# Counts of the bisection steps under the heads: summed by VectorE from a row in HBM instead of by a matmul, with the move behind q and k's low parts

## The chip, the cores and the metric

One core of a Trainium2 chip runs the program. The metric is the device time of one execution in microseconds, the median of several runs. TensorE does matmuls, VectorE and ScalarE elementwise work and reductions along a row, GpSimd casts and splits, SyncE issues most of the DMAs; ScalarE has a DMA queue of its own. Each engine takes its instructions in the order in which they are written, and they meet through semaphores.

## What is computed

```python
x = x + top_k_mask(s * cond * softmax(x) / sqrt(512), diagonal = -inf, k = 5120)   # one 0/1 matrix of 512 x 512 per sequence
ada = (cond @ ada_w + ada_b)                     # shift1, scale1, gate1, shift2, scale2, gate2
x1 = ln(x) * (1 + scale1) + shift1
q, k, v = x1 @ qkv_w + qkv_b                     # 16 heads of 128
a = softmax(q @ k.T / sqrt(128)) @ v @ out_w + out_b
y = x + gate1 * a
y = y + gate2 * (gelu((ln(y) * (1 + scale2) + shift2) @ ffn_w1 + ffn_b1) @ ffn_w2 + ffn_b2)
out = x + y
```

B is 4 sequences of T = 512 rows and D = 512 columns. The mask marks the 5120 largest of the 262,144 values of a sequence.

## The kernel before

The four sequences ("blocks" 0 to 3) are worked one after another: v and then 16 heads of attention, the output projection, and the two layers of the MLP. Every product of float32 is made of three matmuls over high and low parts (`mm3`, L1395 to L1397), so every operand is split in two: on ScalarE the high part is written, on VectorE the low part (`q_hi`, `q_lo` and so on).

In block 0 the weights come raw from HBM (`wraw`), ScalarE casts the high half (L819, `split_hi`), GpSimd makes the low half (L660, `split_lo`), and SyncE saves the pair to `split_weights` in HBM, from which the later blocks load it (L466). In head 3, 7 and 11 of block 0 two more casts than usual stand on ScalarE's queue (`refill`), for the v weights of the next four heads or for the output projection.

**One head h of block b.** TensorE: scores of h (12 matmuls in 4 banks), the total of a bisection step where there is one, the projection of q and k for head h + 1 (24), the v tile of head h + 4 or, from head 12 on, a piece of the output projection, and the product of head h - 1's probabilities with v (`attend`). VectorE: four row maxima (L1217) and biases (L1219), the sums' inverses (L1230, L1232), the low halves of the probabilities (L1236), low parts of q and k for h + 1 (L1187), v's low part (L1182), the low part of head h - 1's output (o, L1187). ScalarE: four exponentials (L883), the probabilities' high halves (L890), q and k (L871, L875), v (L867), o (L910). SyncE turns the halves by DMA transposes (L537), and GpSimd widens them to float32 (L740) for `attend`. All engines go from head to head without a barrier; o of head h - 1 waits for the product, which is the last thing on TensorE in head h, and the first row maximum of h + 1 stands behind it on VectorE.

**The bisection.** The k-th largest value of sequence b + 1 is found under block b, by 32 steps. One step: VectorE counts how many of its half of the keys pass the candidate `cand` (`count`, L1027), ScalarE does so for the other half (`topk_count`, L778), each leaving a number per partition in `counts` (128 x 2). TensorE sums these over the partitions with a matmul against ones (`take_total`, L1411), and VectorE moves the candidate by three small operations (`topk_move`, L1094 to L1099), which both counts of the next step wait for. Steps 0 to 10 (`HEAD_STEPS` is 11) lie under heads 4 to 15: counted at the end of a head, totalled by TensorE behind the scores of the next head, moved by VectorE between that head's biases and its sums. Steps 11 to 31 lie in the stages behind the heads, at places of a table (`SLOTS`); the first of them, `("out", 1, 2)`, is on TensorE shortly behind head 15. The last block has no bisection under it, and block 0's own one runs ahead of all blocks.

## Time and profile before

| | |
|---|---|
| median of 3 runs | 1549.21 us (1548.57 to 1549.74) |
| profiled execution | 1549.28 us, span 1547.5 us |
| TensorE busy | 1499.1 us, 97% |
| VectorE busy | 1107.3 us, 72% |
| ScalarE busy | 884.3 us, 57% |
| GpSimd busy | 424.2 us, 27% |
| DMA | 327.65 MB, mean 212 GB/s |
| granted TensorE clock | 1.00 |

The span is the profiled execution without what lies around it. A head takes about 13.7 us, and 64 heads are more than half of the span. Starts in the rows below are us from the span's start. TensorE's matmuls overlap in the rows: their distance is read from starts, not from durations.

### The profile page before, as it was taken

Reading aid. Unit: us, or ns where it says so; the run is one execution under the profiler, and the core shown is the slowest. Engines: PE = TensorE matmul, PEld = TensorE weight load, DVE = VectorE, ACT = ScalarE, POOL = GpSimd, SP = SyncE. Lnnn points to the kernel's source line nnn. Section 1 sums busy time; section 2 is a strip of 40 time slices with the busy share of each in tenths; the row PEclk is TensorE's granted clock in tenths of the full one; section 3 lists DMA queues with packets and bytes.
Section 4 is the critical chain, followed back from the end, with each engine's and each line's share of the span. In section 5 each row is a group of like instructions: output and inputs, shape, how many; then the busy total and the mean of one; then the engine's idle time right before and its main releaser. Section 6 shows DMA issues by size and latency. Waiting matters only on the chain.

```text
span 1547.5 us, 22147 instructions
## 1 busy us (share of the span) xinstructions
PE 1499.1 (97%) x7157; PEld 1244.7 (80%) x7157; DVE 1107.3 (72%) x2572; ACT 884.3 (57%) x1631; POOL 424.2 (27%) x371
## 2 busy tenths in 40 slices
PE   1999999999999999999999999999999999999998
PEld 1878788879788888888878887888878888888987
DVE  7878887777796887876784887876786666664431
ACT  4656777765846566662753666663572655554340
POOL 6714555554021422331000432232000232223000
PEclk9999999999999999999999999999999999999999
DMA  7866899996767677775465788686465686776463
GB/s 293 300 265 191 230 225 267 255 250 241 257 247 246 172 198 202 207 188 182 172 225 217 196 208 197 155 215 206 164 232 190 191 218 160 196 214 158 182 238 118
DMA packets 338611, 327.65 MB, mean 212 GB/s; under 512 B 274848, under 2 KB 279104, under 8 KB 335424
## 3 DMA queue, kind: packets, MB, share of 16 engines
q1 hardware_dynamic: 338208, 325.91, 71.0%
q8 instruction: 57, 0.93, 0.2%
q14 instruction: 58, 0.48, 0.1%
q10 hardware_dynamic: 288, 0.33, 0.1%
HBM read 204.54 MB, written 54.54 MB: 167 GB/s over the span
## 4 chain that ended last, share of the span: by engine, by line
PE 90%; DVE 4%; DVEq 1%; DMA 1%; ACT 1%; issue 1%; SPq 1%; POOL 0%; ACTq 0%; POOLq 0%
PE bank L1395 27%; PE bank L1397 27%; PE bank L1396 27%; PE bank L1717 2%; PE bank L1615 1%; PE bank L1610 1%; PE bank L1611 1%; DVE tb L1027 1%; PE bank L1427 1%; DVEq L1218 1%; DMA w<-split_weights 1%; SPq L537 1%; PE bank L1449 1%; PE bank L1446 1%; PE bank L1445 1%
## 5 line engine op out<-in xcount | busy, mean ns | idle before, releaser
L740 POOL CAST probT<-turned 128x1024 fp32r<-128x1024 f16 x256 | 260.1, 1053 | 679.5 <-PE bank L1397 355.0
L1395 PE MATMUL bank<-xT,w 128*128 128x512 f32 x704 | 279.7, 397 | 0.0
L1396 PE MATMUL bank<-xT,w 128*128 128x512 f32 x704 | 273.9, 389 | 0.0
L1397 PE MATMUL bank<-xT,w 128*128 128x512 f32 x704 | 273.8, 389 | 0.0
L883 ACT ACTIVATE prob<-bank,nbias 128x512 f32<-128x512 f32 x256 | 176.2, 689 | 107.9 <-DVE nbias L1219 98.8
L1236 DVE SCALAR_TENSOR_TENSOR halves<-prob,rinv,halves 128x512 f16<-128x512 f32 x256 | 176.0, 750 | 27.2 <-ACT halves L890 27.2
L890 ACT ACTIVATE halves<-prob,rinv 128x512 f16<-128x512 f32 x256 | 163.8, 712 | 30.6 <-DVE rinv L1232 23.9
L1217 DVE TENSOR_REDUCE rowmax<-bank 128x1 f32<-128x512 f32 x256 | 174.4, 681 | 0.0
L1397 PEld LDWEIGHTS bank<-xT,w 128*128 128x128 f32 x704 | 132.2, 188 | 28.0
L1395 PEld LDWEIGHTS bank<-xT,w 128*128 128x128 f32 x704 | 132.9, 189 | 25.0
L1396 PEld LDWEIGHTS bank<-xT,w 128*128 128x128 f32 x704 | 132.4, 188 | 24.9
L660 POOL TENSOR_TENSOR w<-wraw,w 128x1024 fp32r<-128x1024 f32 x38 | 94.0, 2478 | 178.8 <-ACT w L819 177.6
L1395 PE MATMUL bank<-act,w 128*128 128x512 f32 (+1 forms) x320 | 113.4, 354 | 0.0
L1397 PE MATMUL bank<-act,w 128*128 128x512 f32 (+1 forms) x320 | 111.0, 347 | 0.0
L1396 PE MATMUL bank<-act,w 128*128 128x512 f32 (+1 forms) x320 | 111.0, 347 | 0.0
L778 ACT ACTIVATE passed_s<-adj,cand 128x1024 bf16<-128x1024 uint16 (+1 forms) x64 | 73.8, 1153 | 62.5 <-DVE cand L1099 37.4
L1187 DVE SCALAR_TENSOR_TENSOR act<-bank,small,act 128x512 fp32r<-128x512 f32 x64 | 47.9, 748 | 85.4 <-ACT act L910 85.4
L910 ACT ACTIVATE act<-bank,small 128x512 fp32r<-128x512 f32 x64 | 44.0, 688 | 106.3 <-PE bank L1397 106.3
L778 ACT ACTIVATE passed_s<-low,cand 128x1024 bf16<-128x1024 f32 (+1 forms) x64 | 74.0, 1156 | 51.0 <-DVE cand L1099 24.1
L1395 PE MATMUL bank<-qk 128*128 128x512 f32 x256 | 100.1, 391 | 1.7 <-DVE qk L1187 1.2
L1395 PE MATMUL bank<-w,act 128*128 128x512 f32 x256 | 101.5, 397 | 0.0
L1187 DVE SCALAR_TENSOR_TENSOR qk<-bank,small,qk 128x512 fp32r<-128x512 f32 x128 | 90.2, 744 | 14.2 <-ACT qk L875 7.9
(171 smaller groups left out, 3314.7 us busy)
## 6 DMA issues: line engine op xcount, KB each, us to landing
w<-split_weights SPq DMA_DIRECT2D x154, 1024.0 KB, 5.6
split_weights<-w SPq DMA_DIRECT2D x38, 1024.0 KB, 6.8
wraw<-weights_in SPq DMA_DIRECT2D x48, 512.0 KB, 4.8
split_weights<-xT SPq DMA_DIRECT2D x7, 1024.0 KB, 8.0
adaw<-ada_w_in SPq DMA_DIRECT2D x4, 1536.0 KB, 13.0
xr<-x_in SPq DMA_DIRECT2D x4, 1024.0 KB, 5.7
turned<-halves SPq DMA_TRANSPOSE x256, 3.3
split_weights<-qk SPq DMA_DIRECT2D x3, 1024.0 KB, 7.6
```

Source lines behind the costliest of these rows:

```text
L660: nc.gpsimd.tensor_tensor(w[:, region, 1, span], wraw[:, k % 2, :], w[:, region, 0, span].bitcast(F32), ALU.subtract)\
L740: nc.gpsimd.tensor_copy(probT[:, :, :, i * P:(i + 1) * P].rearrange("p a j t -> p (a j) t"), turned_of(h)[:, i, :, :]).then_inc(widened, 1)
L778: nc.scalar.activation(passed_s[:, :2 * NCOUNT - at], src, ACT.Sign, bias=cand[:, :], scale=-1.0, accum_out=cnt_s[:, :]).then_inc(counted_ ...
L883: nc.scalar.activation(prob[:, i, :], bank[i][:, :], ACT.Exp, bias=nbias[:, i:i + 1], scale=SCALE, accum_out=rowsum[:, i:i + 1]).then_inc( ...
L890: nc.scalar.mul(halves_of(h)[:, i, 0, :], prob[:, i, :], rinv[:, i:i + 1]).then_inc(p16_hi, 1)
L910: nc.scalar.activation(act[:, 0, h, :], bank[6][:, :], ACT.Identity, bias=col("bv", h))\
L1187: return V.scalar_tensor_tensor(dst, src, bias, hi.bitcast(F32), ALU.add, ALU.subtract)
L1217: V.reduce_max(rowmax[:, i:i + 1], bank[i][:, :], AX.X)
L1236: V.scalar_tensor_tensor(halves_of(h)[:, i, 1, :], prob[:, i, :], rinv[:, i:i + 1], halves_of(h)[:, i, 0, :], ALU.mult, ALU.subtract).then ...
L1395: pe.matmul(dst, w_hi_ap, x_hi_ap, start=first, stop=False)
L1396: pe.matmul(dst, w_hi_ap, x_lo_ap, start=False, stop=False)
L1397: return pe.matmul(dst, w_lo_ap, x_hi_ap, start=False, stop=last)
```

## The change

Under the heads of blocks 0 to 2 the total is no longer a matmul. When both counts of a step are there, ScalarE sends `counts` (128 partitions x 2 numbers of 2 bytes) to a row `count_rows` in HBM, behind head h - 1's o. Behind the exponentials of the next head it waits for that send and fetches the row into all partitions (`all_counts`, 128 x 256 numbers, 512 bytes each). VectorE sums the 256 numbers to two (`summed`), and moves the candidate as before. The move stands no longer between the biases and the sums, but behind q and k's low parts, directly ahead of the count of the next step. TensorE's matmul of the total and its two waits (for o's low part and for the candidate) are gone from the heads. The steps behind the heads stay as they were.

```diff
+        all_counts = at("all_counts", [P, P, 2], F16, passed_at)
+        summed = new("summed", [P, 2], F32)
+        count_rows = nc.dram_tensor("count_rows", (P, 2), F16, kind="Internal").ap()
...
+            def send_counts(t, step):
+
+                act_e.wait_ge(counted_v, t * STEPS + step + 1)
+                act_e.wait_ge(counted_s, t * STEPS + step + 1)
+                act_e.dma_start(count_rows, counts[:, :]).then_inc(counts_out, 16)
+
+            def fetch_counts(t, step):
+
+                act_e.wait_ge(counts_out, 16 * ((t - 1) * HEAD_STEPS + step + 1))
+                act_e.dma_start(all_counts[:, :, :].rearrange("p n c -> p (n c)"),
+                                count_rows.rearrange("n c -> (n c)").unsqueeze(0).to_broadcast([P, 2 * P]))\
+                    .then_inc(counts_in, 16)
...
                     nc.scalar.activation(prob[:, i, :], bank[i][:, :], ACT.Exp, bias=nbias[:, i:i + 1],
                                          scale=SCALE, accum_out=rowsum[:, i:i + 1]).then_inc(exp_done, 1)
+                if not last and h >= FIRST_TOTAL:
+                    fetch_counts(b + 1, h - FIRST_TOTAL)
...
                 if h:
                     o_part(b, h - 1)
+                if not last and 0 <= h + 1 - FIRST_TOTAL < HEAD_STEPS:
+                    send_counts(b + 1, h + 1 - FIRST_TOTAL)
                 refill(b, h, 1)
...
             def topk_move(t, step):
-                dve.wait_ge(total_ready, t * STEPS + (step + 1))
-
+                if is_t0(t):
+                    dve.wait_ge(total_ready, step + 1)
+                    sums = total(step)
+                elif step < HEAD_STEPS:
+                    dve.wait_ge(counts_in, 16 * ((t - 1) * HEAD_STEPS + step + 1))
+                    V.tensor_reduce(summed[:, :], all_counts[:, :, :].rearrange("p n c -> p c n"), AX.X, ALU.add)
+                    dve.drain()
+                    sums = summed
+                else:
+                    dve.wait_ge(total_ready, t * (STEPS - HEAD_STEPS) + step + 1)
+                    sums = total(step)
...
-                if FIRST_TOTAL <= h and not last:
-                    topk_move(b + 1, h - FIRST_TOTAL)
                 keys_first = is_first(b) and 0 < h < FIRST_TOTAL
...
                 if h + 1 < H:
                     qk_part(b, h + 1)
                 dve.drain()
+                if FIRST_TOTAL <= h and not last:
+                    topk_move(b + 1, h - FIRST_TOTAL)
                 if not last and not keys_first:
                     topk_under_head(b + 1, h)
...
-                step = h - FIRST_TOTAL
-                if 0 <= step < HEAD_STEPS and not last:
-                    pe.wait_ge(o_lo, b * H + h)
-                    take_total(b + 1, step)
                 if h + 1 < H:
                     qk_proj(b, h + 1)
...
                 pe.wait_ge(o_lo, b * H + (h + 1))
-                if 0 <= step < HEAD_STEPS:
-                    pe.wait_ge(cand_ready, (b + 1) * (STEPS + 1) + (step + 2))
```

VectorE in a head from 5 on, before: from the last bias to the count.

```order
L1219 TENSOR_SCALAR nbias<-rowmax 128x1
L1094 TENSOR_SCALAR step_up<-bank 128x1 [waits total_ready]
L1097 TENSOR_SCALAR step_up<-bank,step_up 128x1
L1099 TENSOR_SCALAR cand<-cand,step_up 128x1
L1230 TENSOR_SCALAR rowsum<-rowsum 128x1 [waits exp_done]
L1230 TENSOR_SCALAR rowsum<-rowsum 128x1
L1232 RECIPROCAL rinv<-rowsum 128x2
```

The same engine and head after the change, from the sums' inverse to the next row maximum.

```order
L1260 RECIPROCAL rinv<-rowsum 128x2
L1264 SCALAR_TENSOR_TENSOR halves_0_69<-prob,rinv,halves_0_69 128x512 [waits p16_hi] x4
L1217 SCALAR_TENSOR_TENSOR qk<-bank,small,qk 128x512 [waits q_hi]
L1217 SCALAR_TENSOR_TENSOR qk<-bank,small,qk 128x512 [waits k_hi]
L1111 TENSOR_REDUCE summed<-all_counts 128x2 [waits counts_in]
L1124 TENSOR_SCALAR step_up<-summed 128x1
L1127 TENSOR_SCALAR step_up<-summed,step_up 128x1
L1129 TENSOR_SCALAR cand<-cand,step_up 128x1
L1048 TENSOR_SCALAR tb,counts<-adj,cand 128x1024
L1212 SCALAR_TENSOR_TENSOR v<-bank,v 128x512 [waits v_hi]
L1217 SCALAR_TENSOR_TENSOR act<-bank,small,act 128x512 [waits o_hi]
L1247 TENSOR_REDUCE rowmax<-bank 128x1 [waits scores]
```

The three operations of the move now stand behind the low parts of q and k, with a sum of 256 numbers ahead of them, and the count, v's and o's low parts stand behind them.

ScalarE after the change, one head of block 1. Before, the same rows stood there without the two DMA rows.

```order
L931 ACTIVATE act<-bank,small 128x512 [waits pv_done]
L789 DMA count_rows<-counts 128x2 [waits counted_s,counted_v]
L900 ACTIVATE prob,rowsum<-bank,nbias 128x512 [waits nbias_ready] x4
L794 DMA all_counts<-count_rows 128x256 [waits counts_out]
L909 ACTIVATE halves_0_69<-prob,rinv 128x512 [waits turned_in3,turned_in2,rinv_ready,turned_in1,turned_in0]
L909 ACTIVATE halves_0_69<-prob,rinv 128x512 [waits rinv_ready] x3
L888 ACTIVATE qk<-bank,small 128x512 [waits q_done]
L892 ACTIVATE qk<-bank,small 128x512 [waits k_done]
L782 ACTIVATE passed_s,counts<-adj,cand 128x1024 [waits cand_ready]
L884 ACTIVATE v<-bank 128x512 [waits v_done]
```

The send stands behind o and ahead of the exponentials, the fetch between these and the halves; the count (L782) keeps its place on ScalarE, but the candidate that it waits for is now made behind q and k's low parts.

TensorE before, behind the scores of a head; after the change the row of L1411 is gone and the projection follows the scores.

```order
L1395 MATMUL bank<-qk 128x512
L1396 MATMUL bank<-qk 128x512
L1397 MATMUL bank<-qk 128x512
L1411 MATMUL bank<-counts,ones 128x2 [waits counted_s,counted_v,o_lo]
L1395 MATMUL bank<-xT,w 128x512 [waits w_in10]
L1396 MATMUL bank<-xT,w 128x512
```

What moved on this engine: nothing but the total, and the first matmul of `attend` has lost its wait for `cand_ready`.

## Rows read from the trace of the kernel before

**Rows 1.** Part 1 of the page: busy time, share of the span, instructions.

```profile
PE 1499.1 (97%) x7157; PEld 1244.7 (80%) x7157; DVE 1107.3 (72%) x2572; ACT 884.3 (57%) x1631; POOL 424.2 (27%) x371
```

**Rows 2.** Stretches: first score matmul to the next; block 1, twice last; all heads.

```profile
core 0: us, PE busy (x) PEld busy (x) DVE busy (x) ACT busy (x) POOL busy (x), PEclk, DMA share, GB/s
577.35:591.08 13.73, 13.73 (x62) 11.21 (x61) 10.87 (x27) 9.26 (x18) 4.01 (x4) 1.00 0.62 150
1284.53:1298.13 13.60, 13.60 (x61) 11.27 (x60) 9.18 (x22) 8.00 (x16) 4.01 (x4) 1.00 0.66 165
1366.13:1379.05 12.92, 12.92 (x58) 10.70 (x57) 8.49 (x21) 7.40 (x15) 4.01 (x4) 1.00 1.04 307
484.60:685.17 200.57, 200.57 (x890) 164.46 (x889) 164.45 (x405) 133.48 (x266) 59.92 (x60) 1.00 0.76 198
119.11:324.97 205.86, 202.35 (x890) 163.88 (x889) 167.86 (x405) 150.64 (x287) 109.62 (x81) 1.00 0.93 239
```

**Rows 3.** Timeline of TensorE around a total: start, duration, engine, line, operation.

```profile
579.84 0.39 PE L1397 MATMUL bank<-qk 128*128 128x512 f32 x1
...
580.43 0.39 PE L1396 MATMUL bank<-xT,w 128*128 128x512 f32 x1
```

**Rows 4.** Timeline of VectorE, head 7 of block 1.

```profile
587.07 1.41 DVE L1187 SCALAR_TENSOR_TENSOR qk<-bank,small,qk 128x512 fp32r<-128x512 f32 x2
588.59 1.28 DVE L1027 TENSOR_SCALAR_CACHE_REDUCE tb<-adj,cand 128x1024 bf16<-128x1024 uint16 x1
```

**Rows 5.** Timeline of VectorE and ScalarE, head 7 of the last block.

```profile
1299.72 0.68 DVE L1217 TENSOR_REDUCE rowmax<-bank 128x1 f32<-128x512 f32 x1
...
1303.84 2.55 ACT L890 ACTIVATE halves<-prob,rinv 128x512 f16<-128x512 f32 x4
...
1307.24 1.41 DVE L1187 SCALAR_TENSOR_TENSOR qk<-bank,small,qk 128x512 fp32r<-128x512 f32 x2
```

**Rows 6.** Timeline of VectorE and ScalarE, a move behind the heads.

```profile
702.66 0.16 DVE L1094 TENSOR_SCALAR step_up<-bank 128x1 f32<-128x1 f32 x1 [2.06 <-PE bank L1411]
...
703.44 1.15 ACT L778 ACTIVATE passed_s<-adj,cand 128x1024 bf16<-128x1024 uint16 x1 [2.97 <-DVE cand L1099]
```

**Rows 7.** DMAs: issue on ScalarE's queue; size, median us to landing.

```profile
0.79 0.39 ACTq L993 DMA_DIRECT2D small<-cols_in  x1
...
turned<-halves SPq DMA_TRANSPOSE x256, 3.3
...
small<-cols_in ACTq DMA_DIRECT2D x1, 64.0 KB, 1.8
gate_rows<-gate_t SPq DMA_DIRECT2D x1, 16.0 KB, 5.9
```

**Rows 8.** Timeline, block 0: TensorE's wait in head 4, heads 5 and 7, v tile.

```profile
184.06 0.50 PE L1395 MATMUL bank<-w,xT 128*128 128x512 f32 x1 [1.77 <-POOL w L660]
...
196.39 0.72 ACT L890 ACTIVATE halves<-prob,rinv 128x512 f16<-128x512 f32 x1 [1.71 <-DMA turned<-halves]
199.96 0.74 DVE L1187 SCALAR_TENSOR_TENSOR qk<-bank,small,qk 128x512 fp32r<-128x512 f32 x1
200.94 1.15 ACT L778 ACTIVATE passed_s<-adj,cand 128x1024 bf16<-128x1024 uint16 x1
203.96 0.68 DVE L1217 TENSOR_REDUCE rowmax<-bank 128x1 f32<-128x512 f32 x1
...
228.26 1.05 ACT L819 CAST w<-wraw 128x1024 fp32r<-128x1024 f32 x1
231.73 4.01 POOL L740 CAST probT<-turned 128x1024 fp32r<-128x1024 f16 x4
235.70 2.40 POOL L660 TENSOR_TENSOR w<-wraw,w 128x1024 fp32r<-128x1024 f32 x1
239.17 0.39 PE L1395 MATMUL bank<-w,xT 128*128 128x512 f32 x1
```

**Rows 9.** Timeline of VectorE and TensorE behind head 15 of block 1.

```profile
696.57 0.09 DVE L1027 DVE_READ_ACCUMULATOR tb<-adj,cand 128x1 f16 x1
...
698.23 0.18 PE L1411 MATMUL bank<-counts,ones 128*128 128x2 f16 x1
```

More of the change, by code:

```diff
@@ L373, in block_kernel @@
                                                        sem("adj_ready"), sem("diag_done"))
+        counts_out, counts_in = sem("counts_out"), sem("counts_in")
         cand_ready, counted_v, counted_s, total_ready = (sem("cand_ready"), sem("counted_v"),
@@ L1084, in topk_move @@
             def topk_move(t, step):
-                dve.wait_ge(total_ready, t * STEPS + (step + 1))
+                if is_t0(t):
[9 more added lines that the diff above has]
+                    sums = total(step)
                 bit = TOP_BIT / (1 << step % LEVEL)
                 if is_t0(t):
-                    move = V.tensor_scalar(cand[:, :], total(step)[:, 0:1], bounds[:, 0:1], bounds[:, 1:2],
+                    move = V.tensor_scalar(cand[:, :], sums[:, 0:1], bounds[:, 0:1], bounds[:, 1:2],
                                            ALU.max, ALU.min)
@@ L1093, in topk_move @@
                     bit *= unit(step)
-                    V.tensor_scalar(step_up[:, :], total(step)[:, 1:2], 0.5, float(KTOP - P * NCOUNT // 2) - 0.5,
+                    V.tensor_scalar(step_up[:, :], sums[:, 1:2], 0.5, float(KTOP - P * NCOUNT // 2) - 0.5,
                                     ALU.mult, ALU.add)
                     dve.drain()
-                    V.tensor_scalar(step_up[:, :], total(step)[:, 0:1], step_up[:, :], bit, ALU.is_gt, ALU.mult)
+                    V.tensor_scalar(step_up[:, :], sums[:, 0:1], step_up[:, :], bit, ALU.is_gt, ALU.mult)
                     dve.drain()
@@ L1527, in head, with attend @@
                 if h:
-                    attend(b, h - 1, step if not last else -1)
-            def attend(b, h, step):
+                    attend(b, h - 1)
+            def attend(b, h):
                 q, m = h // QUAD, h % QUAD
@@ L1679, in sequence @@
                 wide(b, "out", 0, KC - 2, KC - 1, y_done)
-                attend(b, H - 1, -1)
+                attend(b, H - 1)
                 wide(b, "out", 2, 0, 3, y_done)
```

## The prediction

> **What bounds the kernel now.** I read the page first: TensorE is busy 97% of the span [rows 1], so a removal counts only where it takes time out of TensorE's row of matmuls, and a delay elsewhere costs only once TensorE waits for it. Then the stretches of single heads [rows 2]. A head of block 1 takes 13.73 us from one first score matmul to the next, and TensorE is busy in all of it. The same head in the last block, where no bisection runs under the heads, takes 13.60. Sixty matmuls of 0.2265 us (the distance of starts) are 13.59, so the last block is TensorE at its pace. The difference of 0.13 to 0.14 us is the total: between the matmul before it (579.84) and the second one behind it (580.43) lie 0.59 us, where two plain steps are 0.45 [rows 3]. Heads 12 to 14, three matmuls shorter, take 12.92 without totals. The granted clock is 1.00 in all these stretches.
>
> **What the change takes away.** 3 blocks x 11 heads (5 to 15) lose one total each: 33 x 0.135 = 4.5 us, all on TensorE's own path. The waits of TensorE for the counts and for the candidate in these heads go too; block 1's heads have no idle time of TensorE [rows 2], so they are worth nothing.
>
> **What it adds, and where it lies.** I follow one loop, from a head's first rowmax to the next head's first rowmax on VectorE, since VectorE and ScalarE take turns on it.
> Rowmax to the low parts of q and k: the last block has no move there and shows 1299.72 to 1307.24, 7.52 us, with ScalarE's halves starting 4.12 behind the rowmax [rows 5]. So with the move gone from its old place the halves of all heads come that early.
> Low parts to the next VectorE instruction: 587.07 to 588.59, 1.52 [rows 4].
> The new sum of 256 numbers: not in the trace. Below, a 128x1 operation is 0.16 [rows 6]; above, a reduction of 512 is 0.68 [rows 5]. I take 0.44 with the handover, half the elements of the upper row and its fixed part.
> Move until ScalarE's count starts: 702.66 to 703.44, 0.78 [rows 6].
> Count on ScalarE, then v, o, and VectorE's rowmax of the next head, with no wait for TensorE among them: 200.94 to 203.96, 3.02 [rows 8].
> Sum 7.52 + 1.52 + 0.44 + 0.78 + 3.02 = 13.28 us, against the 13.60 that TensorE takes. The margin is 0.32 (0.60 to 0.08 over the bounds of the sum): where nothing else comes, the longer loop hides under the matmuls. A head that starts late also has a cushion: TensorE wants q and k's low parts of head 8 at 591.08 and has them at 588.48, 2.6 us early [rows 2, 4].
>
> The two DMAs. The send is queued behind o on ScalarE and ahead of the next exponentials; behind it in the queue stand these, the fetch, the halves. From o to the halves there are about 5.5 us (1.4 with o's low part, the end of the 3.02 above, then 4.12). The two issues were 0.39 us each where ScalarE's queue was otherwise empty [rows 7]; the exponentials last until 0.1 before the halves, so the issues can lie under them if ScalarE's arithmetic goes on while its queue issues. Issue to landing for the 512 bytes: 1.8 us is the lowest row, 3.3 the transposes under the same load, 5.9 the worst small one, queued behind others [rows 7]. I take 3 to 3.5, inside the window of 4.7; likewise the fetch has some 5 us until the sum. So: nothing in blocks 1 and 2.
> The Trainium skill, "Advanced Engine Details and Errata", section Sequencer Loop, says that other engine instructions can be read and queued while the sequencer executes a control instruction. No row of this trace shows a DMA issued by ScalarE beside its arithmetic; by that page the issues are free, and the other answer is the third case below.
>
> **Block 0 is another matter.** Its heads take 205.86 us where block 1 takes 200.57 [rows 2], because ScalarE also casts weights and GpSimd splits them, and the loop arrives late. In head 5 the halves start only at 196.39, held by transposes; low parts follow at 199.96, and ScalarE counts at 200.94, beside them [rows 8]. After the change the count stands behind them and the move: 199.96 + 1.52 + 0.44 + 0.78 = 202.7, 1.76 later. The next rowmax is at 205.7 instead of 203.96, and 0.32 a head gives back little. Head 7: rowmax 219.0, count at 229.3, and the cast of the first half of the next v weights behind v, 1.6 later, at 230.9 instead of 228.26 [rows 8]. Follow it: cast done 231.9, GpSimd's split 2.4 to 234.4, its four casts of probT (before from 231.73) 4.0 to 238.4, the split of the second half (before from 235.70) to 240.8. TensorE asks for that half at 239.17, and with four totals gone at 238.6: 2.2 us of waiting that are not there now. The trace has such a wait once, at 184.06, 1.77 us for the same splits [rows 8]. Heads 11 to 14 repeat the pattern (two casts at head 11, transposes queued behind the weights' loads); there the boundaries are late already, and I take 2.4 us for both together, an estimate from the same lags. Last, the first total behind the heads: in block 1 the counts are done at 696.66 and TensorE comes at 698.23 [rows 9], 1.57 of cushion. Without a lag the new order takes 0.57 of it (the move only changes its place, the sum's 0.44 is new, TensorE comes 0.13 sooner). A lag of about 2.1 us in block 0 then costs 1.1. Block 0: 2.2 + 2.4 + 1.1 = 5.7 us lost.
>
> **The sum** against the profiled run, 1549.28 us (span 1547.5; median of the runs 1549.21): -4.5 + 5.7 = +1.2, **1550.5 us**.
>
> **Rivals.**
> *The gain stays (22%).* If head 5's late start is made good (GpSimd splits in another order of arrival, raw loads land earlier), block 0 loses nothing: 1549.3 - 4.5 = 1544.8. For it: TensorE's row shows no other cost, blocks 1 and 2 have 2.6 us of cushion. Against it: the cast at 230.9 is a plain sum of rows.
> *The issues are not hidden (27%), slower.* If each fetch takes 0.42 us from ScalarE before the halves, the loop is 13.70, above 13.60, and decides from there: VectorE falls back in every head. In blocks 1 and 2 the lag grows by 0.10 in heads 5 to 11 and by 0.3 in heads 12 to 14, whose loop loses only the v part (0.5) while TensorE's stretch loses 0.68 [rows 2]: 1.6 us, within the cushion of 2.6 but not within that of the first total behind the heads: 1.6 + 0.42 - 1.0 is 1.0 us each, 2 in all. In block 0 three heads' issues come on top before each pair of casts and at the end, 3.6 us. Together 1550.5 + 5.6 = 1556.
> The skill's page "Perfetto Trace Analysis", section DMA Instruction (HWDGE), says that one descriptor generator is shared by the issuing sequencers and locked while it is used. SyncE's transposes take 5.5 us of issue for four in every head, so by this page the same case would come from a send or fetch that meets them; no row shows two queues issuing at once.
> *The send lands late (9%).* ScalarE stands at the fetch until the rows have landed, with halves and q, k behind it. From 4.7 us of landing on, each further microsecond is one per head: at 2 us too late 33 x (2 - 0.3) less three times the cushion of 2.6 is 48 us, some 1598. For it speaks only the row of 5.9.
> *Forecast (42%)*, 1548 to 1554 with the bounds of the sum (0.08 to 0.60 of margin) and of block 0's 2.4.
>
> **Range and chances.** A measurement of this kernel can tell about 0.2%, 3.1 us. Faster by more is the first rival, 0.22; within is the forecast, 0.42; slower are the other two, 0.36. The range from 1544 to 1561 takes in the first rival and most of the second, and leaves out about 0.15.
>
> **What would show it.** Head stretches of blocks 1 and 2 of 13.60 and 12.92 us: the total's price is right. ScalarE's halves 4.1 us behind the rowmax, not 4.5 or more: the issues are hidden; an idle time of the halves put down to a DMA to count_rows is the late landing. Idle time of VectorE before the sum would be a late fetch. A gap of 2 us before a v matmul near 239 us, put down to GpSimd's w: block 0's account. I am wrong if block 0 keeps its 205.9 less 1.5, or if the sum takes over 0.76 us with its handover, since the margin is then gone in every head.

## The result: 11.6% slower, and the time is in the send

| | before | after |
|---|---|---|
| median, us | 1549.17 | 1728.56 (1722.99 to 1733.53) |
| span of the profiled run, us | 1547.5 | 1731.5 |
| mean granted clock of TensorE | 1.000 | 0.958 |

The ratio is 1.1155, 95% interval 1.1139 to 1.1172: some 180 us, where 1 was forecast and the range ended 12 above the time of before. In the page of the kernel after, these lines answer to [rows 1] and [rows 7] (busy time; the chain of what ended last, by engine and by line; a group of instructions with what ended its idle time; DMA issues with their median landing):

```profile
PE 1553.3 (90%) x7124; PEld 1280.3 (74%) x7124; DVE 1127.7 (65%) x2605; ACT 884.1 (51%) x1631; POOL 427.9 (25%) x371
...
PE 58%; DMA 21%; DVE 10%; SPq 4%; ACT 2%; DVEq 2%; issue 2%; ACTq 0%; POOL 0%; POOLq 0%
...
L909 ACT ACTIVATE halves<-prob,rinv 128x512 f16<-128x512 f32 x256 | 163.7, 712 | 162.9 <-DMA count_rows<-counts 101.1
...
all_counts<-count_rows ACTq DMA_DIRECT2D x33, 64.0 KB, 5.0
...
count_rows<-counts ACTq DMA_DIRECT2D x33, 0.5 KB, 9.8
```

TensorE's share fell from 97% to 90%, and DMAs make up 21% of the chain (1% before). The send's median landing is 9.8 us, its shortest 7.8; the forecast had taken 3 to 3.5. ScalarE's halves (the high halves of the probabilities) stood idle for 162.9 us (30.6 before), 101.1 of them put down to the send, in 20 of the 33 heads, and 52.3 to transposes of the halves before them (6.7 before). The transposes' median landing is 3.4 us (3.3 before), the longest 14.6 (8.2 before). In the view of stretches, the heads of block 1, single heads of it, the stretch behind them, and the last block (us, TensorE busy, ..., granted clock):

```profile
core 0: us, PE busy (x) PEld busy (x) DVE busy (x) ACT busy (x) POOL busy (x), PEclk, DMA share, GB/s
625.55:642.71 17.16, 13.76 (x62) 11.11 (x60) 9.10 (x23) 8.00 (x16) 4.01 (x4) 1.00 0.45 104
676.87:700.78 23.91, 18.64 (x60) 14.14 (x61) 13.66 (x34) 10.37 (x20) 4.18 (x4) 0.79 1.04 201
560.27:807.08 246.81, 214.48 (x881) 172.90 (x879) 167.37 (x410) 132.03 (x264) 60.77 (x60) 0.94 0.79 162
807.08:975.99 168.91, 162.59 (x825) 135.36 (x826) 113.08 (x243) 79.59 (x132) 11.25 (x12) 0.97 0.58 190
1389.64:1588.88 199.24, 199.24 (x881) 164.98 (x880) 134.74 (x326) 117.26 (x236) 56.31 (x56) 1.00 0.77 200
```

Block 1's heads went from 200.57 us [rows 2] to 246.81; the last block, which sends nothing, is at its pace. A head of 17.16 us has 3.4 us in which TensorE is idle. In the head of 23.91 it is also slower: 60 matmuls keep it busy for 18.64 us at a granted clock of 0.79, behind heads in which it had stood idle, where 62 took 13.73 at 1.00 before. Over the run TensorE's busy time grew by 54 us (1499.1 to 1553.3, with 33 matmuls less) and its time outside that by 130. The three stretches behind the heads, in which nothing is sent, are 28.7 us of the 184 by which the span grew (169.29, 168.91 and 168.87 us against 159.63, 159.26 and 159.48). In each of them TensorE stands idle once for what the last head left late, 6.3, 6.1 and 6.4 us (the first total behind the heads, and in block 2 the probabilities), and is busy for some 3 us more than before at a granted clock of 0.97.

What one head waits for, in the timeline of ScalarE and VectorE in head 7 of block 1 (start, duration; idle time ahead of an instruction and what ended it in brackets):

```profile
662.06 0.58 ACT L884 ACTIVATE v<-bank 128x512 fp32r<-128x512 f32 x1
662.32 0.33 ACTq L789 DMA_DIRECT2D count_rows<-counts  x1
...
667.96 0.19 ACT L900 ACTIVATION_READ_ACCUMULATOR prob<-bank,nbias 128x1 f32 x1
671.42 0.33 ACTq L794 DMA_DIRECT2D all_counts<-count_rows  x1
671.95 1.34 ACT L909 ACTIVATE halves<-prob,rinv 128x512 f16<-128x512 f32 x2 [3.80 <-DMA count_rows<-counts]
...
675.36 1.41 DVE L1217 SCALAR_TENSOR_TENSOR qk<-bank,small,qk 128x512 fp32r<-128x512 f32 x2
676.86 0.42 DVE L1111 TENSOR_REDUCE summed<-all_counts 128x2 f32<-128x256 f16 x1
677.36 0.15 DVE L1124 TENSOR_SCALAR step_up<-summed 128x1 f32<-128x1 f32 x1
```

The send goes out at 662.32 and the fetch can be issued only at 671.42, 9.1 us later; the exponentials have been done since 668.15. The loop behind the landing is as forecast: low parts to the sum 1.50 (1.52), sum and handover 0.50 (0.44). The send is issued while ScalarE computes v, and costs it nothing.

So the place of the loss is plain. Why 512 bytes take 9 us, and whether that wait is the whole loss, is not.

### The profile page after: what moved, and what is told of

Same layout as the page of the kernel before. It is cut to its first block, busy times and chain, and to the rows that moved or that the text cites. A ratio compares the mean times of both kernels' runs of the same rounds, so it can differ in the third digit from the quotient of the medians.

```text
span 1731.5 us, 22204 instructions
## 1 busy us (share of the span) xinstructions
PE 1553.3 (90%) x7124; PEld 1280.3 (74%) x7124; DVE 1127.7 (65%) x2605; ACT 884.1 (51%) x1631; POOL 427.9 (25%) x371
## 4 chain that ended last, share of the span: by engine, by line
PE 58%; DMA 21%; DVE 10%; SPq 4%; ACT 2%; DVEq 2%; issue 2%; ACTq 0%; POOL 0%; POOLq 0%
PE bank L1425 17%; PE bank L1426 16%; PE bank L1427 16%; DMA count_rows<-counts 14%; SPq L541 3%; DVE halves L1264 3%; DMA w<-split_weights 2%; DMA turned<-halves 2%; DVE tb L1048 2%; PE bank L1741 2%; ACT halves L909 1%; DMA all_counts<-count_rows 1%; DMA wraw<-weights_in 1%; PE bank L1639 1%; PE bank L1634 1%
## 5 line engine op out<-in xcount | busy, mean ns | idle before, releaser
L909 ACT ACTIVATE halves<-prob,rinv 128x512 f16<-128x512 f32 x256 | 163.7, 712 | 162.9 <-DMA count_rows<-counts 101.1
L1425 PE MATMUL bank<-qk 128*128 128x512 f32 x256 | 109.3, 427 | 62.5 <-DVE qk L1217 62.0
L782 ACT ACTIVATE passed_s<-adj,cand 128x1024 bf16<-128x1024 uint16 (+1 forms) x64 | 74.0, 1157 | 147.3 <-DVE cand L1129 122.1
L1425 PE MATMUL bank<-probT,v 128*128 128x512 f32 x256 | 107.0, 418 | 27.8 <-POOL probT L744 27.7
L1425 PE MATMUL bank<-act,w 128*128 128x512 f32 (+1 forms) x320 | 116.3, 363 | 12.8 <-DMA w<-split_weights 12.8
L1426 PE MATMUL bank<-act,w 128*128 128x512 f32 (+1 forms) x320 | 113.6, 355 | 0.0
L1427 PE MATMUL bank<-act,w 128*128 128x512 f32 (+1 forms) x320 | 113.5, 355 | 0.0
L1425 PEld LDWEIGHTS bank<-qk 128*128 128x128 f32 x256 | 52.1, 204 | 82.1 <-DVE qk L1217 70.8
L1426 PE MATMUL bank<-qk 128*128 128x512 f32 x256 | 107.2, 419 | 0.0
L1427 PE MATMUL bank<-qk 128*128 128x512 f32 x256 | 107.0, 418 | 0.0
L1426 PE MATMUL bank<-probT,v 128*128 128x512 f32 x256 | 105.5, 412 | 0.0
```

The source lines that it names most:

```text
L782: nc.scalar.activation(passed_s[:, :2 * NCOUNT - at], src, ACT.Sign, bias=cand[:, :], scale=-1.0, accum_out=cnt_s[:, :]).then_inc(counted_ ...
L909: nc.scalar.mul(halves_of(h)[:, i, 0, :], prob[:, i, :], rinv[:, i:i + 1]).then_inc(p16_hi, 1)
L1425: pe.matmul(dst, w_hi_ap, x_hi_ap, start=first, stop=False)
L1426: pe.matmul(dst, w_hi_ap, x_lo_ap, start=False, stop=False)
L1427: return pe.matmul(dst, w_lo_ap, x_hi_ap, start=False, stop=last)
```

## The experiments

### Is it the place of the move? Or the DMAs? (move_only, free_dmas, fetch_late, bench)

*move_only* is the kernel before, with the move in its new place and the total still a matmul, copied out of PSUM at the old place:

```diff
-                    topk_move(b + 1, h - FIRST_TOTAL)
+                    copy_total(b + 1, h - FIRST_TOTAL)
...
+                if FIRST_TOTAL <= h and not last:
+                    topk_move(b + 1, h - FIRST_TOTAL)
                 if not last and not keys_first:
                     topk_under_head(b + 1, h)
```

> The move alone stands behind the low parts of q and k; the total stays TensorE's matmul at its old place, copied out of PSUM by one small VectorE operation at the move's old place, and no DMA is added. Theory A (the time lies in the wait for the send's landing): within 0.5% of the kernel before, 1545 to 1556 us, with block 0 alone slower by 2 to 6 us. Theory B (the later move and count make VectorE and ScalarE's loop longer than TensorE's head): clearly slower in every head from 5 on, 1570 us or more.

Measured: 1551.53 us against 1549.66, ratio 1.0013 (1.0004 to 1.0022). The move's place costs 2 us, so theory B falls.

*free_dmas* is the kernel before with DMAs on which nothing depends: constants sent, and fetched late in the next head.

```diff
+                act_e.dma_start(count_rows[n], ones[:, 0:2]).then_inc(counts_out, 16)
...
+                if not last and h >= FIRST_TOTAL:
+                    fetch_counts(b + 1, h - FIRST_TOTAL)
                 if h:
                     o_part(b, h - 1)
+                if not last and 0 <= h + 1 - FIRST_TOTAL < HEAD_STEPS:
+                    send_counts(b + 1, h + 1 - FIRST_TOTAL)
```

> The kernel before, with a send of 128 x 4 bytes to HBM and a fetch of 512 bytes to all partitions per head as in the change, but of constants, into a row of its own per step; no engine's work needs them: the fetch is issued late in the next head. Theory A (a wait, not the traffic): 1547 to 1553 us, the sends still 8 us or more to landing. Theory C (128 small descriptors each slow the transposes and the weights' loads on the shared DMA engines): 1570 us or more, with transposes well above 3.4 us to landing.

Measured: 1720.68 us, ratio 1.1104 (1.1082 to 1.1126). This was the surprise of the study: nearly the whole loss, though no count is waited for. In the waits of this kernel the same halves now wait for something else, their own transposes:

```profile
L540 SPq DMA_TRANSPOSE turned<-halves x256: 1230/1247/5494, 127.1 to 1584.9; - x128
...
  POOL probT L744: 592.3, 70
  ACT halves L909: 147.9, 25
...
DMA to landing us min/median/max: 3.0/3.6/16.6
```

The second and third lines tell who waited for the transposes, how long in all and how often. Before, ScalarE's halves waited for them 6.7 us in all and the longest landing was 8.2.

*fetch_late* is the change with only ScalarE's wait and fetch moved, from ahead of the halves to ahead of the next count:

> The change with only the fetch moved on ScalarE, from ahead of the probabilities' halves to ahead of the count. Theory A in the form that halves, q and k waiting behind the fetch are what costs: most of the 180 us come back, under 1600 us. Theory A' (the send's 8 to 9 us, the fetch's 3 to 5, sum, move and count are one chain longer than a head wherever the fetch stands): 1690 to 1760 us, the halves again 4.1 us behind the rowmax, and the idle time before VectorE's sum instead.

Measured: 1719.12 us, ratio 1.1093 (1.1070 to 1.1116). The 101 us of the halves' wait are gone (they wait 30.7 for transposes) and 139.5 us of VectorE's wait for all_counts stand in their place. Moving the wait does not help. It doesn't tell what late counts cost by themselves, since the slow sends and their hold on the transposes are in this run too.

*bench* leaves out all of the reference's work and times single DMAs on ScalarE's queue, each landing waited for, on a quiet chip, beside loads of 1 MB, and beside transposes. All three of the following send 128 pieces of 4 bytes: `near` side by side in HBM, `far` 512 bytes apart, `row` into one partition's row in SBUF.

```diff
+                    act_e.dma_start(dram["near", ph], counts[:, :]).then_inc(sems["near", ph], 16)
...
+                    act_e.dma_start(dram["far", ph][:, 0:2], counts[:, :]).then_inc(sems["far", ph], 16)
...
+                    act_e.dma_start(dst["row", ph][0:1, :].rearrange("o (n c) -> o n c", c=2), counts[:, :])\
```

> Measures DMAs of ScalarE's queue by themselves, one at a time, each waited for, six times each: 128 x 4 bytes to one dense row in HBM (near), the same at 512 bytes' distance (far), 128 x 512 bytes to HBM (wide), 128 x 4 bytes into a row of one SBUF partition (row), that row to HBM in one piece (one), and a row of HBM into all partitions (all). First with no other traffic (quiet), then beside loads of 1 MB by SyncE (loads), then beside DMA transposes (turns). All of the reference's work is left out; the output is a copy of x. Theory L (load): near takes 2 to 3 us when quiet and 8 or more beside loads. Theory S (size and target: writes of 4 bytes to one line of HBM): near takes 6 us or more even when quiet, far and row clearly less.

Measured, from the view of its DMAs (median us to landing last):

```profile
near_quiet<-counts ACTq DMA_DIRECT2D x6, 0.5 KB, 7.2
far_quiet<-counts ACTq DMA_DIRECT2D x6, 0.5 KB, 1.4
row_quiet<-counts ACTq DMA_DIRECT2D x6, 0.5 KB, 1.9
...
near_loads<-counts ACTq DMA_DIRECT2D x6, 0.5 KB, 10.8
far_loads<-counts ACTq DMA_DIRECT2D x6, 0.5 KB, 7.8
...
near_turns<-counts ACTq DMA_DIRECT2D x6, 0.5 KB, 8.3
far_turns<-counts ACTq DMA_DIRECT2D x6, 0.5 KB, 1.9
```

The same 128 pieces of 4 bytes land in 7.2 us side by side and in 1.4 when 512 bytes lie between them. Number, size and queue are the same in both: it is where the pieces fall. Load adds 1 to 4 us to the near ones. The far ones aren't always quick either: beside the loads of 1 MB they take 7.8 us, beside the transposes 1.9.

### Which DMA costs, and by what? (sends_only, fetches_only, far_sends, row_route)

The first three are free_dmas with one thing altered. *sends_only* drops the fetches; *fetches_only* keeps the first send alone and fetches its row 33 times; *far_sends* writes every send but the first 512 bytes apart (the fetches of both read the first row).

```diff
-                act_e.dma_start(count_rows[n], ones[:, 0:2]).then_inc(counts_out, 16)
+                act_e.dma_start(far_rows[n][:, 0:2] if n else count_rows[0], ones[:, 0:2]).then_inc(counts_out, 16)
```

> The kernel before with 33 sends of a constant (128 writes of 4 bytes to a dense row of 512 bytes in HBM) on ScalarE's queue where the change sends the counts, ScalarE waiting for the landing late in the next head; nothing is fetched, the totals are the matmul's. Theory L (the small writes themselves are slow, 8 to 13 us, and the turned<-halves transposes that are issued while they are under way land late with them, which holds GpSimd's probT and ScalarE's halves): 1700 to 1725 us, nearly all of what sends and fetches cost together (1720.68), with transposes landing up to 14 to 17 us after their issue. Rival F (the fetch, 128 rows of 512 bytes, is what the others wait for): 1550 to 1570. Rival W (nothing is held on the DMA side, ScalarE's own wait for the landing is what costs): about 1720 too, but transposes would land within 8.2 us as in the kernel before.

> The kernel before with one send at the first step and 33 fetches of that row to all partitions (64 KB each) where they stood beside the matmul totals; nothing depends on what they bring. Theory L: 1549 to 1556 us, transposes as before (median 3.3, longest about 8 us). Rival F: 1690 to 1720.

> The kernel before with the 33 sends and 33 fetches on which nothing depends, but each send writes its 128 pieces of 4 bytes 512 bytes apart, not side by side. Alone on a quiet chip such a send landed in 1.4 us, against 7.2 for the dense row. Theory L (slow because all pieces fall in one 512-byte stretch): 1550 to 1570 us. Rival Y (any 128 small pieces on a second queue disturb the transposes, wherever they go): 1690 to 1720 like the dense ones.

Measured: sends_only 1706.07 us (ratio 1.1011, 1.0979 to 1.1043), fetches_only 1554.39 (1.0033, 1.0022 to 1.0045), far_sends 1555.43 (1.0036, 1.0020 to 1.0052). The dense sends alone cost 156 us. The fetches cost 5, the fetches together with as many sends to another pattern of addresses 6, and most of even that comes with one dense send: both kernels keep the first, and in block 0, where it goes out at 188.77 us in far_sends, ScalarE's halves come late behind it:

```profile
188.77 0.34 ACTq L790 DMA_DIRECT2D count_rows<-ones  x1
201.25 0.72 ACT L910 ACTIVATE halves<-prob,rinv 128x512 f16<-128x512 f32 x1 [6.58 <-DMA turned<-halves]
```

That head takes 19.0 us from exponential to exponential, where it took 13.5; the heads of its blocks 1 and 2 take what they took before. In sends_only the same happens in head after head. Block 1 again, GpSimd's casts of the turned halves and ScalarE:

```profile
666.52 0.33 ACTq L788 DMA_DIRECT2D count_rows<-ones  x1
...
669.38 1.04 POOL L743 CAST probT<-turned 128x1024 fp32r<-128x1024 f16 x1 [0.39 <-DMA turned<-halves]
678.14 1.04 POOL L743 CAST probT<-turned 128x1024 fp32r<-128x1024 f16 x1 [7.71 <-DMA turned<-halves]
...
678.16 2.56 ACT L903 ACTIVATE halves<-prob,rinv 128x512 f16<-128x512 f32 x4 [6.40 <-DMA turned<-halves]
```

Three of the head's four transposes have landed; the fourth, issued about when the send was, lands 11.6 us behind the send's issue. GpSimd's cast and ScalarE's next halves, which write the tile that it reads, wait for it. Of the theories on record, L holds: what is under way beside the dense send is held with it. F and Y fall. So does W, since transposes land up to 15.3 us after their issue, not within 8.2, and ScalarE's own wait for the sends is 1.1 us in the whole run.

*row_route* is the change with the counts sent to one partition's row in SBUF first, from there in one piece to HBM, then fetched:

```diff
-                act_e.dma_start(count_rows, counts[:, :]).then_inc(counts_out, 16)
+                act_e.dma_start(count_row[0:1, :].rearrange("o (n c) -> o n c", c=2), counts[:, :])\
+                    .then_inc(row_made, 16)
...
+                act_e.dma_start(count_rows.rearrange("n c -> (n c)").unsqueeze(0), count_row[0:1, :])\
+                    .then_inc(counts_out, 16)
```

> The change with another way for the counts: sent first to one partition's row in SBUF (128 pieces of 4 bytes), from there in one piece of 512 bytes to HBM (issued between the exponentials), then fetched by all partitions as in the change. Theory L: the transposes land as before, the three landings (about 3.4, 1.9 and 4 us) reach the sum at most about 3 us late, so 1555 to 1600 us. Rival Y (the small pieces disturb wherever they go): above 1690. If both the place of the pieces and their number matter, something between.

Measured: 1611.45 us, ratio 1.0400 (1.0363 to 1.0437), 11 above the top of what was expected: the row send's median landing is 4.8 us in the kernel, not 3.4. The transposes land as before (median 3.3, longest 8.2), and ScalarE's halves wait for none of them. What is left is that three landings in a row are too long for a head: ScalarE waits 30.6 us for the first (18 times) and its halves 28.4 us for the second (12 times).

### Where is the limit, and does it hold others up by itself? (bench2, bench3)

> None of the reference's work (out is a copy of x). First, on a quiet chip, ScalarE's queue writes 128 pieces of 4 bytes, one from each partition, to a row in HBM with the pieces 4, 8, 16, 32, 64, 128, 256 and 512 bytes apart, each landing waited for. Theory L (what is slow is that many pieces fall in one 512-byte stretch): the landing falls stepwise with the spacing, from 7.2 us at 4 bytes towards 1.4 at 512, with 3 to 5 us at 16 to 32 bytes. Rival R (only a shared word or a partly written 64 bytes is slow): everything from 64 bytes on is alike at about 1.4 us, everything below about 7. Then SyncE issues 40 transposes of 128x1024 two deep: alone, beside a chain of sends to the dense row, and beside a chain of sends 512 bytes apart; and the same with loads of 1 MB. Theory L: transposes 3.2 us alone and beside the far sends at most 4, but beside the dense sends a median of 5 to 8 us and more in the longest; loads 6 to 7 us alone and 1 to 3 us more beside the dense sends. Rival Q (transposes are held only where other loads are in flight too): transposes beside the dense sends alone stay near 3.3.

*bench2* first wrote the 128 pieces at eight distances, five times each, one send behind the other. From one issue to the next, which is little more than the landing, it took 7.0 to 8.3 us at 4 bytes, 2.7 to 3.2 at 8, 1.4 to 2.5 at 16 (1.4 in three of five), and 1.4 to 2.0 from 32 bytes on. So there is no step at 512 bytes, where theory L had put it, and none at 64, where R had.

Then it issued 40 transposes two deep, then 12 loads of 1 MB two deep: alone, beside a chain of dense sends, beside a chain of sends 512 bytes apart. SyncE's issues (start, and the us from the first issue to the last):

```profile
218.50 63.67 SPq L294 DMA_TRANSPOSE turn_alone<-hv  x40
284.10 110.67 SPq L294 DMA_TRANSPOSE turn_beside_near<-hv  x40
396.69 64.89 SPq L294 DMA_TRANSPOSE turn_beside_far<-hv  x40
463.52 34.80 SPq L296 DMA_DIRECT2D wb<-src_load_alone  x12
504.91 69.51 SPq L296 DMA_DIRECT2D wb<-src_load_beside_near  x12
601.04 30.00 SPq L296 DMA_DIRECT2D wb<-src_load_beside_far  x12
```

Eight dense sends of 512 bytes add 47 us to 40 transposes and double the time of the loads (the median load lands in 13.6 us, not 6.8). The 24 far sends add 1.2 us to the transposes and nothing to the loads. Rival Q falls, since no load is needed beside the transposes. Theory L had the median of the transposes wrong: it stays at 3.3 us, since eight sends meet only some of the 40, and those land up to 11.7 us after their issue.

> None of the reference's work (out is a copy of x). On a quiet chip, 128 pieces, one from each partition, of 4, 8, 16, 32 and 64 bytes lying side by side in HBM, and pieces of 4 bytes every 8, 16 and 32 bytes (earlier: 7 us side by side, 2.9, 2.1 and 1.9). Theory N (what costs is two pieces that share 8 bytes: the memory is written 8 bytes at a time or more, one after the other): 8 bytes side by side lands in about 2.9 us and 16 in about 2.1, like pieces of 4 bytes at those distances. Theory Z (every piece of under 64 bytes costs the same read and write back, and only the distance decides): the same figures. Theory B (the small piece itself is slow, whatever lies beside it): 8 bytes side by side 2.9 or more, 16 side by side under 2. If pieces of 8 and 16 bytes side by side are as slow as those of 4 (6 to 8 us), it is the touching, not the distance. Beside them, 24 transposes of 128x1024 two deep take about 38 us alone: 50 to 66 beside the 4 bytes side by side, and 38 to 42 beside the others.

*bench3*, pieces from 128 partitions, by size and distance:

```profile
four_side_by_side<-counts ACTq DMA_DIRECT2D x6, 0.5 KB, 7.5
eight_side_by_side<-counts ACTq DMA_DIRECT2D x6, 1.0 KB, 2.9
sixteen_side_by_side<-counts ACTq DMA_DIRECT2D x6, 2.0 KB, 1.4
...
four_every_eight<-counts ACTq DMA_DIRECT2D x6, 0.5 KB, 2.8
four_every_sixteen<-counts ACTq DMA_DIRECT2D x6, 0.5 KB, 1.5
four_every_thirtytwo<-counts ACTq DMA_DIRECT2D x6, 0.5 KB, 1.4
```

Size makes no difference (4 bytes every 8 are as fast as 8 side by side), nor does touching, and since 4 bytes every 16 land in 1.5 us, this run's theory B falls. What counts is the distance of the pieces' starts: 7.5 us at 4 bytes, 2.9 at 8, about 1.4 from 16 on. Theories N and Z give the same figures and aren't told apart. Every send had 128 pieces, so the distance and the length of the whole stretch grow together here, and fewer pieces weren't tried.

The transposes beside them did not go as expected. From the first to the last issue, 24 of them take 70.4 us beside six sends side by side (50 to 66 expected), with medians of 5.5 and 5.1 us to landing and the longest over 10, and 46.0 beside eight sends 8 bytes apart (38 to 42 expected), with landings up to 6.2. Beside ten sends 16 bytes apart they take 39.9, and beside ten of 16 bytes side by side 39.3. So pieces 8 bytes apart still hold others, only less.

### The change without its slow send (apart16, apart8)

The same kernel as the change, with the pieces 16 (or 8) bytes apart; the fetch brings the gaps along, and the sum reads every fourth (second) pair. SyncE fills the row once at the start, so that the gaps hold numbers.

```diff
-        all_counts = at("all_counts", [P, P, 2], F16, passed_at)
+        all_counts = at("all_counts", [P, P, 8], F16, passed_at)
...
-                act_e.dma_start(count_rows, counts[:, :]).then_inc(counts_out, 16)
+                act_e.dma_start(count_rows[:, 0:2], counts[:, :]).then_inc(counts_out, 16)
```

> The change with one thing altered: the 128 pieces of 4 bytes lie 16 bytes apart in HBM, not side by side, so the fetch brings 2 KB to each partition (256 KB, landed in 3.2 us alone) and VectorE sums every fourth pair. Alone such a send landed in 2.1 us, against 6.9 to 7.5 side by side. If the send's landing was the one step of the forecast that failed, its other steps hold here: a landing of up to 4.7 us from the low parts costs nothing, the fetch has about 5 us, 33 heads win 0.135 us each and block 0 loses about 6: 1549 to 1558 us, heads 5 to 14 of blocks 1 and 2 at a pace of 13.6 us as in the last block, transposes as before. If the length of the route itself (two landings in a row) is too long for a head, whatever the spacing: 1575 to 1620, as with the route through SBUF (1611).

> The same with pieces 8 bytes apart: alone the send landed in 2.9 us, the fetch of 1 KB to each partition in about 3. If the landing alone decides: 1549 to 1565 us, at most some us above the one with 16 bytes. If pieces that share a few bytes' neighbourhood still hold the transposes: 1580 or more, with transposes over 9 us.

Measured: apart16 1566.35 us, ratio 1.0105 (1.0088 to 1.0122); apart8 1585.37, ratio 1.0226 (1.0184 to 1.0268). One number of the layout takes back 162 of the 179 us. Both lie above what was expected, by 8 and 20 us (apart8 has two runs only, 10 us apart, 1580.15 and 1590.58). With 8 bytes the send lands in 5.0 us in the kernel, not 2.9, and late transposes still hold the halves a few times (5.0 us in all, the longest landing 8.9).

In most heads of apart16 the loop can at last be seen as it was forecast. Head 6 of block 2 as a stretch, and ScalarE and VectorE in it:

```profile
939.54:953.14 13.60, 13.60 (x61) 11.26 (x60) 11.68 (x29) 9.13 (x20) 4.00 (x4) 1.00 0.72 178
```

```profile
940.00 0.33 ACTq L791 DMA_DIRECT2D count_rows<-counts  x1
...
941.58 0.68 DVE L1249 TENSOR_REDUCE rowmax<-bank 128x1 f32<-128x512 f32 x1
...
945.07 0.33 ACTq L796 DMA_DIRECT2D all_counts<-count_rows  x1
...
945.68 2.55 ACT L911 ACTIVATE halves<-prob,rinv 128x512 f16<-128x512 f32 x4
...
950.58 0.60 DVE L1113 TENSOR_REDUCE summed<-all_counts 128x2 f32<-128x256 f16 x1
...
952.03 1.15 ACT L784 ACTIVATE passed_s<-adj,cand 128x1024 bf16<-128x1024 uint16 x1 [2.65 <-DVE cand L1131]
...
955.06 0.68 DVE L1249 TENSOR_REDUCE rowmax<-bank 128x1 f32<-128x512 f32 x1
```

The halves start 4.10 behind the rowmax, with a fetch issued under the exponentials; nothing in this head waits for a landing; TensorE is busy in all of 13.60 us, where it took 13.73. The loop from rowmax to rowmax is 13.48.

## Why the prediction was wrong, point by point

**The step that failed** is the send's landing: "I take 3 to 3.5, inside the window of 4.7". It was 8 to 13 us. The bounds were rows of one 64 KB load in large pieces, transposes, and a small save of 16 KB; none of these writes pieces 4 bytes apart, and the one of 5.9, already beyond the window, was put aside as queued. On a quiet chip the send takes 7.2, so no reading of the load could have saved the step.

**The third rival had the wait, at 9%, and half of the mechanism.** It said that an idle time of the halves put down to count_rows would show it, and 101.1 us of that are there. Its price was for 2 us too late; by its own rule, (9.8 - 4.7 - 0.3) x 33 less its 7.8 us, the time would be 1550.5 + 151 = 1701. That this comes near 1728.56 is in part luck: the halves wait for counts in 20 heads, not 33, and the rule leaves out the other half of the mechanism. The send holds the transposes and loads beside it, and costs 156 us even where nobody wants the counts (sends_only). Late counts and held transposes together cost 179, so the counts add 23 at most. Late counts with the transposes as before are in row_route only, at 62 us, and there they come by another way; what a wait for a landing of 9.8 us would cost by itself is not shown.

**The total's price, 0.135 a head, is right.** apart16 has heads of 13.60 and 12.92 us; but 0.135 x 33 is 4.5 us, and nothing else in the change is seen to give time back.

**The loop of 13.28 is right.** In the kernel after, its parts are 1.50, 0.50 and about 0.77, against 1.52, 0.44 and 0.78. In apart16 the strided sum takes 0.60 instead of 0.42, and the loop is 13.48, still under 13.60. In heads 13 and 14, which have no v, it is 12.97 to 13.14 in blocks 1 and 2, against TensorE's 12.92: VectorE can fall behind there by up to 0.2 us a head.

**The fetch's window is a second step that failed, a smaller one.** The forecast gave the fetch "some 5 us until the sum" and no price. In the kernel after its median landing is 5.0 us, and VectorE's sum waits for it 14.2 us in all, in 10 heads. In apart16, where it brings 2 KB to each partition, the median is 3.7 but the longest 7.0; the sum waits 7.2 us in all, in 6 heads, in head 12 of blocks 1 and 2 for 1.50 and 1.44. In apart8 it waits 15.7 us, in 13 heads. In block 1, and TensorE's wait for the first total behind its heads:

```profile
671.16 0.60 DVE L1113 TENSOR_REDUCE summed<-all_counts 128x2 f32<-128x256 f16 x1 [1.50 <-DMA all_counts<-count_rows]
...
713.00 0.16 PE L1443 MATMUL bank<-counts,ones 128*128 128x2 f16 x1 [2.42 <-DVE tb L1050]
```

From that head on VectorE is late: in blocks 1 and 2 the first rowmax of head 15 stands 3.9 us behind its score matmuls where it stood 1.6. The three stretches behind the heads grow from 159.63, 159.26 and 159.48 us to 162.5, 163.3 and 162.0. That is 9.4 of the 16.8 us by which apart16's span is longer, 6.9 of them TensorE's waits for the first total (2.0, 2.4 and 2.5); the forecast had 1.1 for it, in block 0 alone. The heads of blocks 1 and 2 together are 1.4 us shorter than before, where it had 3. Of the missing 1.6 us, 1.4 are a wait of TensorE for a weights' load in head 8 of block 1; what made that load late isn't shown.

**The issues are hidden**, so the second rival (27%) falls. The send's row at 662.32 lies inside v's, and in apart16 the fetch's, at 945.07, inside the last exponential. This is what the Trainium skill, "Advanced Engine Details and Errata", section Sequencer Loop, leads one to expect. The lock on the shared descriptor generator that the Trainium skill describes in "Perfetto Trace Analysis", section DMA Instruction (HWDGE), and on which that rival leaned, is not seen as a cost here. In fetches_only the fetch of 580.56 is issued in 0.36 us in the midst of four transposes that SyncE issues from 577.20 to 582.74; the 33 fetches leave the heads of blocks 1 and 2 no longer than they were, and a transpose's median issue at 1.25 us.

**Block 0's 5.7 us** can't be read from the kernel after, where the landing covers it. In move_only its heads take 209.3 us by exponentials instead of 206.0. In apart16 they take 212.80 by score matmuls instead of 205.86, 6.9 more, where the forecast's items for the heads give 3.1 net of the totals. The chain that was forecast for the v weights is there. The cast behind v starts at 233.63, 1.3 us behind head 8's first score matmul, where before it started 1.3 ahead of it: 2.5 later, against 2.6 forecast. Then GpSimd's split and TensorE:

```profile
241.06 2.36 POOL L666 TENSOR_TENSOR w<-wraw,w 128x1024 fp32r<-128x1024 f32 x1
243.47 0.50 PE L1427 MATMUL bank<-w,xT 128*128 128x512 f32 x1 [1.42 <-POOL w L666]
```

TensorE waits 1.42 us, against 2.2 forecast. Heads 12 and 13 are 3.2 and 1.0 longer, the first with a wait of TensorE for q's low part of 3.17, where 2.4 had been taken for both of the later places. Head 4 is 1.5 longer, head 9 0.7, for reasons that stay open. That leaves 1.8 us of apart16 ahead of the first head. They need not be the change's: far_sends and sends_only, whose instructions are the same up to there, differ by 1.4 at that point (119.14 and 120.55).

**The range** ended at 1561, since the bounds of the unknown landing stopped short of where the case with the highest price began, and 9% was put on a case whose only argument against it was the choice of a row.

## What to carry to other kernels

A DMA's cost is not told by its bytes: look at how far apart its pieces fall in HBM, and before you route something small through it, time that very pattern, alone and beside the loads that it will meet. An added DMA that nobody waits for can still cost 10% when it holds others up; a kernel with that DMA and with nothing depending on it shows that in one run. And where a removal is worth 0.135 us a head, a longer loop in its place has to stay below the shortest head, not the usual one, and a DMA in it has to fit its window by its longest landing, not by its median.

## What the hardware showed that I had not expected

- 128 writes of 4 bytes that lie side by side in HBM took 7.2 to 7.5 us (medians) on a quiet chip and 9.8 in this kernel; 8 bytes apart 2.7 to 3.2, from 16 bytes on 1.4 to 2.5. Beside loads of 1 MB even pieces 512 bytes apart took 7.8.
- While such a send is under way, DMAs of another queue are held: 8 of them made 40 transposes take 110.67 us instead of 63.67, and 12 loads of 1 MB 69.51 instead of 34.80. Pieces 8 bytes apart still did so, less.
- The same pieces into one partition's row in SBUF took 1.9 us alone, and in row_route, where they took 4.8, the transposes landed as before (longest 8.2).
- No version here beats the kernel before. The best with the new route is apart16 at 1566.35 us; since the removed totals are worth 4.5 us in all and the longer loop costs more behind the heads, there looks to be little left to find on this way.
